# A graph layer's edge scores: scattered after one wait in four pairs, kept for all pairs, and the next pair's one-hots turned ahead of this pair's row sums

## The reference

```python
xl = (x @ W_l).reshape(N, HEADS, HEAD_DIM)
xr = (x @ W_r).reshape(N, HEADS, HEAD_DIM)
e = xl[src] + xr[dst]
e = jnp.where(e >= 0, e, NEG_SLOPE * e)
score = jnp.einsum('ehd,hd->eh', e, att)
m = jax.ops.segment_max(score, dst, num_segments=N)
ex = jnp.exp(score - m[dst])
alpha = ex / (denom[dst] + SM_EPS)
agg = jax.ops.segment_sum(alpha[:, :, None] * xl[src], dst, num_segments=N)
```

## Time and profile before

| | |
|---|---|
| time, median of 3 runs | 1112.62 us (1112.42 to 1114.56) |
| profiled execution | 1119.57 us, its span 1117.8 us |
| PE busy | 862.5 us, 77% of the span |
| DVE busy | 766.6 us, 69% |
| POOL busy | 375.2 us, 34% |
| ACT busy | 352.7 us, 32% |
| scatters (L2243) | 184, 226.6 us busy, 1232 ns each; first at 113.5 us, last at 474.7 us |

### The profile page before, as it was taken

One profiled execution on the slowest core, in us unless ns is written; L12 is line 12 of the kernel. 1 busy time (PEld: TensorE's weight loads), 2 busy tenths in 40 slices (PEclk: granted clock), 3 DMA queues, 4 the chain that ended last, 5 costly groups with the idle time before them and its releaser, 6 DMA issues.

```text
span 1117.8 us, 18660 instructions
## 1 busy us (share of the span) xinstructions
PE 862.5 (77%) x5483; PEld 736.2 (66%) x5483; DVE 766.6 (69%) x1980; ACT 352.7 (32%) x1096; POOL 375.2 (34%) x321
## 2 busy tenths in 40 slices
PE   4889679699888881017639999895896787699996
PEld 3578567588766660017538999783586476689895
DVE  7778777855777771028977888577788755766635
ACT  0277434273455553015401111101362062112120
POOL 3287646455677666500002222150000000211104
PEclk9988888699899996558858999996898798699999
DMA  8830000000000000089028999970000000688893
GB/s 282 256 119 1 3 2 3 2 3 2 3 3 4 4 2 3 2 195 229 25 65 282 313 321 318 349 231 23 1 1 1 0 2 14 242 300 296 302 328 95
DMA packets 38282, 129.39 MB, mean 116 GB/s; under 512 B 12885, under 2 KB 20929, under 8 KB 29913
## 3 DMA queue, kind: packets, MB, share of 16 engines
q1 hardware_dynamic: 21742, 112.64, 30.8%
q0 software_dynamic: 10464, 8.67, 4.5%
q10 hardware_dynamic: 5992, 7.04, 1.8%
HBM read 108.83 MB, written 19.26 MB: 115 GB/s over the span
## 4 chain that ended last, share of the span: by engine, by line
PE 57%; DVE 18%; DMA 11%; issue 7%; POOL 4%; ACT 2%; DVEq 0%; POOLq 0%; SPq 0%; ACTq 0%
PE bank L854 12%; PE bank L643 9%; PE bank L865 6%; DMA arena<-pair_scores 4%; PE bank L582 4%; PE bank L787 3%; DMA pair_scores<-sc_ring,pair_cells 2%; PE bank L621 2%; PE bank L623 2%; POOL arena L2277 2%; POOL pair_scores L2243 2%; DMA arena<-slot_y,sloti 2%; PE bank L953 2%; PE bank L622 2%; PE bank L653 2%
## 5 line engine op out<-in xcount | busy, mean ns | idle before, releaser
L2243 POOL DMA_INDIRECT pair_scores<-sc_ring,pair_cells x184 | 226.6, 1232 | 144.5 <-issue 70.8
L2267 POOL DMA_INDIRECT arena<-row_tab,ids x42 | 57.5, 1369 | 501.6 <-DVE ids L1660 494.2
L854 PE MATMUL bank<-arena 128*128 128x128 f32 x1480 | 180.6, 280 | 2.6 <-DMA arena<-in_exp 2.6
L854 PEld LDWEIGHTS bank<-arena 128*128 128x128 f32 x1480 | 174.7, 196 | 4.8 <-DMA arena<-in_exp 4.0
L643 PE MATMUL bank<-x_hi,hot 125*125 x368 | 119.9, 346 | 17.4 <-ACT tc L2007 9.9
L1997 ACT ACTIVATE hot<-bank 125x250 fp32r<-125x250 f32 x184 | 68.8, 379 | 163.8 <-PE bank L623 163.5
L776 PE MATMUL bank<-ident,arena 125*125 125x125 f32 x260 | 44.9, 306 | 85.3 <-ACT arena L2054 84.1
L1273 DVE TENSOR_TENSOR tc<-tc,vec 125x512 f32<-125x512 f32 x92 | 64.0, 696 | 56.8 <-ACT tc L2007 56.8
L643 PE MATMUL bank<-x_lo,hot 125*125 x368 | 102.8, 299 | 0.0
L643 PEld LDWEIGHTS bank<-x_hi,hot 125*125 125x125 f32 x368 | 73.1, 199 | 44.4 <-issue 43.7
L865 PE MATMUL bank<-arena 128*128 128x256 f32 (+1 forms) x404 | 99.1, 389 | 2.9 <-issue 2.9
(11 more groups left out here) (397 smaller groups left out, 1747.0 us busy)
## 6 DMA issues: line engine op xcount, KB each, us to landing
arena<-in_exp SPq DMA_DIRECT2D x25, 1024.0 KB, 7.1
arena<-in_exp SPq DMA_DIRECT2D x17, 1386.0 KB, 6.3
arena<-in_exp0o SPq DMA_DIRECT2D x25, 512.0 KB, 7.2
pair_scores<-cnt SPq DMA_DIRECT2D x10, 1093.8 KB
arena<-in_exp1o SPq DMA_DIRECT2D x17, 640.0 KB
arena<-pair_scores SPq DMA_DIRECT2D x7, 1093.8 KB
slot_y<-arena ACTq DMA_DIRECT2D x34, 128.0 KB, 6.4
fmaps<-pair_scores SPq DMA_DIRECT2D x3, 1093.8 KB
```

The costliest lines, as they stand in the source:

```text
L854: mm = pe.matmul(banks[1 + 2 * q + buf][0:rows, i * SLOTS:(i + 1) * SLOTS], w_in(s, q, k, m, rows), xsT[:, s, k, :], start=(k == 0), stop= ...
L2243: p.indirect_dma_start(out=pair_scores[which], in_=sc_ring[:, i % SCORED, which, :], in_offset=None, out_offset=bass.IndirectOffsetOnAxis( ...
L2267: p.indirect_dma_start(out=xs[:, q, :], out_offset=None, in_=tab, in_offset=bass.IndirectOffsetOnAxis(ap=ids[:, q, :], axis=0))\
```

## The change

It does three things.

- POOL's wait for scores: a pair's even scatter awaited `scored` in all 92 pairs. Now it does so in pairs 0 to 3, each for itself, and from then on only in pairs 4, 8, ..., 88, where it waits for the scores of the whole four that begins there. The waits on `scattered0` and `scattered1` stay.
- `sc_ring` has a place for each of the 92 pairs and lies in the arena, behind `w_by_att`, in memory that the sorting used earlier. DVE's two waits for the landing of an earlier pair go.
- PE turns columns 2i+2 and 2i+3 ahead of `sum_rows(i)`.

```diff
-SCORED = 16
+SCORED = PAIRS
+AHEAD = 4
...
-                sum_rows(i)
                 for c in (2 * i + 2, 2 * i + 3):
                     if c < SORTED:
                         turn_hots(c)
+                sum_rows(i)
                 mix(i)
...
             def score(i):
 
-                for w in range(2):
-                    after(dve, sem(f"scattered{w}"), 16 * (i - SCORED + 1))
                 own.fence()
...
-                if which == 0:
-                    pool.wait_ge(sem("scored"), i + 1)
+                if which == 0 and (i < AHEAD or i % AHEAD == 0):
+                    pool.wait_ge(sem("scored"), i + 1 if i < AHEAD else min(i + AHEAD, PAIRS))
                 after(pool, sem(f"scattered{which}"), 16 * i)
```

More of the change, by code:

```diff
@@ L255, in build @@
         by_head = sb("by_head", [P, T, 2, H])
-        sc_ring = sb("sc_ring", [P, SCORED, 2, H])
         cnt = sb("cnt", [P, T, N])
@@ L270, in build @@
         slot_parts = arena[0:P, at:at + BUCKETS * EC].rearrange("p (b j) -> p b j", b=BUCKETS)
+        sc_ring = arena[0:P, at + K2 * 2 * D:at + K2 * 2 * D + SCORED * 2 * H].rearrange("p (s c h) -> p s c h", s=SCORED, c=2)
         w_by_att = arena[:, at:at + K2 * 2 * D].rearrange("p (k n) -> p k n", k=K2)
@@ L1276, in score @@
             def score(i):
-                for w in range(2):
-                    after(dve, sem(f"scattered{w}"), 16 * (i - SCORED + 1))
                 own.fence()
-                v.tensor_reduce(sc_ring[:, i % SCORED, :, :].rearrange("p c h -> p (c h)"),
+                v.tensor_reduce(sc_ring[:, i, :, :].rearrange("p c h -> p (c h)"),
                                 weighed[:, i % 2, :, :, :].rearrange("p c h d -> p (c h) d"), AX.X, ALU.add)\
@@ L2239, in scatter @@
                 which, i = c % 2, c // 2
-                if which == 0:
-                    pool.wait_ge(sem("scored"), i + 1)
+                if which == 0 and (i < AHEAD or i % AHEAD == 0):
+                    pool.wait_ge(sem("scored"), i + 1 if i < AHEAD else min(i + AHEAD, PAIRS))
                 after(pool, sem(f"scattered{which}"), 16 * i)
                 p.indirect_dma_start(
-                    out=pair_scores[which], in_=sc_ring[:, i % SCORED, which, :], in_offset=None,
+                    out=pair_scores[which], in_=sc_ring[:, i, which, :], in_offset=None,
                     out_offset=bass.IndirectOffsetOnAxis(ap=pair_cells[:, c:c + 1], axis=0))\
```

## The result

The changed kernel takes 1157.88 us (median of 4 runs, 1154.14 to 1161.9) beside 1113.06 us before: a ratio of 1.040 (1.037 to 1.043), slower by 44.8 us. The forecast was 1115.6, its range ended at 1127. The profiled execution took 1161.9 us, its span is 1160.1 (before 1117.8).

The account below looks back on a forecast made before the run. POOL's scatter pace from pair 40 was taken to bound the stage, ending at 478.8 us; +9.2 - 14 + 0.3 + 7.5 = +3.0 us on the median 1112.62 gave 1115.6 us, range 1107.5 to 1127.

Parts of the forecast that it names:

- part 4: PE turning ahead of row sums: they enter the PE-ACT-DVE cycle, 0.5 us a pair more, +7.5 us by pair 43.
- a rival: PE's clock falls to the lower level; half of the loop so gives +18 us, 1130.7 us; chance 0.15.
- the cover behind POOL: After pair 43, POOL's backlog hides 7 us of slower scores, 0.15 us a pair; beyond that DVE sets the end.
- 18.9 us behind the last score: Stage's end when DVE sets it: time from the last score to the end, 18.9 us.
- Part 1: POOL's even scatters without the second wait: pairs take 2.98 instead of 3.42 us from pair 40 to 87, -14 us.
- Part 2: POOL's wait for four pairs at once: pair 40's scatter waits for pair 43's score, +9.2 us.
- Last four pairs: End of POOL's scatters: late landings set the pace in both kernels, 18.6 instead of 18.3 us, +0.3 us.
- Part 3: Ring of 92 and DVE's dropped waits for landings 16 pairs back: cost and gain nothing.
- The delay of pair 43: Score of pair 43 on DVE: 17 of the first 44 pairs have the longer cycle, +7.5 us, bounds 0 and 9.5.
- the mixing pieces were to cover the new cycle: Among the first 44 pairs, those led by PE's or DVE's mixing work lose nothing to the longer cycle.
- The forecast's own case: All terms together with PE's clock at the upper level: +3.0 us, 1115.6 us; chance 0.55.

Follow-up runs that it names:

- half-sums kernel: Kernel before without the four row-sum matmuls a pair that read x_lo, part of the computation missing: 1105.22 us, ratio 0.9930.
- POOL's parts alone: Changed kernel with PE's old order, row sums ahead of both turnings; one wait in four and ring of 92 stay: 1114.61 us, ratio 0.9985.
- the ring alone: Kernel before with sc_ring's 92 places in the arena and without DVE's two waits, nothing else: 1113.22 us, ratio 1.0007.
- the fours from 52: Changed kernel with PE's old order and POOL's one wait in four pairs only from pair 52 on: 1104.86 us, ratio 0.9938.
- three fillers: Changed kernel plus three unread 500-column matmuls between PE's two turnings, in pairs 0 to 8 and 41 to 90: 1127.41 us, ratio 1.0094.
- one filler: Changed kernel plus one unread 500-column matmul between PE's two turnings, in pairs 0 to 8 and 41 to 90: 1120.61 us, ratio 1.0068.
- the even column: Kernel before with only column 2i+2 turned ahead of pair i's row sums, column 2i+3 behind them: 1122.78 us, ratio 1.0064.

## Why the prediction was wrong, point by point

**The step that failed is the clock in part 4**: the sum prices a pair at +0.5 us with PE at 1.00, and leaves the low clock to a rival with a chance of 0.15 and the size "if half of the loop ran so", +18 us. The premise was read from rows: 2.39 us of work over 3.24 is 74% busy, and the one row with such a share had a clock of 0.90. Two things were wrong with that. The 2.39 us of the earlier trace rows are the profile's busy time, in which pipelined matmuls overlap what follows; a pair's fourteen matmuls follow each other by 0.12, some 1.7 us, and the half-sums kernel shows how little the profile's share says: 90% busy, clock 0.50. And the one row was taken from another stage with other matmuls: 47 in 8 us, where a loop of 3.24 us a pair has 35, and with two waits, not one in every period. What the runs showed: all of the pairs from 43 on at 0.50, not half of them, 0.85 us a pair (forecast "some 0.9"). The price per pair was right; how many pairs pay it was not. With the rival's own price for all 48 pairs the end would have been 424.9 + 7.5 + 48 x 1.4 + 18.9 = 518.5; 519.5 was measured. That this is so close is luck in part: pair 43 was 10.3 us later than in that sum, and a pair grew by 1.23, not 1.4.

**How the failed step turned into 40 us.** The prediction itself said that the cover behind POOL is 7 us, 0.15 us a pair, and decides "from 0.15 us a pair on". The last score should have come at 456.4 and came at 500.4. Then DVE sets the end, and the wait for four pairs, which costs nothing when scores lie ahead, puts a whole four behind the last score. The prediction had named this, "18.9 us behind the last score"; 19.1 were measured. The agreement is luck: the last four took 16.5 us, not 18.6, and POOL came to them only 2.7 us after the last score, because the four before them had been held for pair 87.

- Part 1, -14 us: mechanism right (0.29 instead of 0.82 us behind a landing, 1.49 between scatters). Against the profiled execution of before the size is nearly right: from pair 40 to pair 88 POOL took 175.3 us there and 162.4 with POOL's parts alone, 12.9 less. Against the ring alone (169.9), at equal median to before, it is only 7.5 less, and the fours from 52 take 6.6 less. So the term was nearly twice too large. Of the 36 pairs that lose the wait 19 took the forecast 2.98 us; late landings held the others, and the mean was 3.30, not the 3.03 that 1.8 us taken off would give.
- Part 2, +9.2 us: right. Pair 40's scatter starts 9.3 us later with the fours from the start.
- Last four pairs, +0.3 us: right while POOL sets the pace (18.3 us in both profiles, so 0); in the changed kernel DVE sets it, and the fours cost 8.7 us at the end.
- Part 3, 0: right.
- Part 4, the chain: 3.24 us forecast, 3.12 and 3.11 measured at the full clock, 3.97 at the low one. The turnings and row sums took a little less than the links added up. The delay of pair 43 was mis-sized: 7.5 us forecast, 17.8 measured. With three fillers it is still 11.4, with one 14.4. Pair 9 is already 8.9 us late, and the clock of 112 to 136 us falls from 0.91 to 0.57. Between pair 9 and pair 40, where the mixing pieces were to cover the new cycle and no filler stands, the changed kernel loses another 6.7 us, while the clock of 160 to 300 us falls from 0.89 to 0.84. I had read the clock of the mixing pairs as given.
- The forecast's own case, with the clock kept up, would have been the kernel with one filler: ratio 1.0068, some 7.6 us slower; 3 us were forecast. The sign was right; pair 43 comes 14.4 us late instead of 7.5, which is more than the difference.

The Trainium skill, page "TensorE: Matmul & The Clock Gate", section "Part 1: The HAM clock gate", says that activity releases the throttle; the fillers agree (0.50 to 1.00 by one more matmul a pair). The prediction left open whether gaps of some 1.3 us bring the clock down; here gaps of 1.24 us once a pair, with this work between them, go with 0.50 for 192 us.

**What stays open.** How the fall of the clock in the changed kernel divides between the length of PE's gap and the work between the gaps: the fillers change both, the half sums mostly the work, the even column mostly the gap, and both lowered the clock.

## What to carry to other kernels

Before moving a wait on PE, add up the matmuls' own steps in one period and look at the longest gap that the new order leaves: a loop that idles once per period can sit at half the clock, as this one did, and then every link of the cycle that runs on PE must be priced at the low level. In these runs the low clock cost something a pair only where PE's work lay in the cycle, so keep row sums beside the chain rather than in it; a thrown-away matmul can prove the cause in one run. A wait for several items at once is free only while the consumer is behind by that many: start it where the backlog is (pair 52 here, 0.6% faster than before), not where the consumer keeps pace.

## What the hardware showed that I had not expected

- The granted clock stayed at 0.50 for 192 us in a loop in which PE is 69% busy by the profile and never idles over 1.24 us; one more matmul of 500 columns in each 3.1 us brought it to 1.00 from 304 to 450 us.
- More work on PE made the kernel faster by 37 us; half of the row sums left out made PE *busier* by the profile (90%) at a clock of 0.50.
- With the same work a pair and the idle time in one piece of 0.6 us, the clock was 0.87 to 0.91 instead of 1.00.
- The end of a stage of indirect DMAs differs by 6.6 us between profiled executions of kernels with equal medians.
